# Scan stage: the step size's sums on GpSimd, two-source small VectorE steps, and a product of H and C that waits for its own scan

## What is computed

```python
x = L0_attn_x
x = x + 0.5 * _L0_ffn_ref(_layernorm(x, axis=-1), ...)
x = x + _L0_attn_ref(_layernorm(x, axis=-1), ...)
x = x + 0.5 * _L0_ffn_ref(_layernorm(x, axis=-1), ...)
x = x + 0.5 * _L1_ffn_ref(x, ...)
x = x + _L1_attn_ref(_layernorm(x, axis=-1), ...)
x = x + 0.5 * _L1_ffn_ref(x, ...)
```

```python
dt = jnp.einsum('blr,dr->bld', dt_low, W_dt)
delta = jax.nn.softplus(dt + b_dt)
A = -jnp.exp(A_log)

def step(h, inp):
    dlt_t, B_t, C_t, x_t = inp
    dA = jnp.exp(dlt_t[:, :, None] * A)
    h = h * dA + dlt_t[:, :, None] * B_t[:, None, :] * x_t[:, :, None]
    y_t = jnp.einsum('bdn,bn->bd', h, C_t)
    return (h, y_t)
```

## Time and profile before

| | us |
|---|---|
| times of three runs | 3141.8, 3126.4, 3141.92 |
| median | 3141.8 |
| span of the profiled execution | 3131.4 |
| scan stage, about | 1590 to 2772 |
| VectorE busy, whole span | 2073.9 |
| GpSimd busy, whole span | 1699.2 |
| TensorE busy, whole span | 2457.7 |

### The profile page before, as it was taken

How to read it: one execution, slowest core, us unless ns; L and a number is a source line. 1 busy time by engine, 2 the same in 40 slices (tenths; PEclk the granted TensorE clock), 3 DMA queues, 4 the chain that set the end, 5 groups by cost and what they waited for, 6 DMA issues and landing times. The chain is left out here.

```text
span 3131.4 us, 49074 instructions
## 1 busy us (share of the span) xinstructions
PE 2457.7 (78%) x12952; PEld 1742.2 (56%) x12952; DVE 2073.9 (66%) x6083; ACT 1589.5 (51%) x3093; POOL 1699.2 (54%) x1349
## 2 busy tenths in 40 slices
PE   4239996885799844399979888888888889769991
PEld 4239994664699733299933333333343334349991
DVE  6414445775444455155539999999999999955553
ACT  3115554773355443155545666666656666425550
POOL 5745550455355447555515566776666667645551
PEclk9999997996899976699989999999999999879996
DMA  9147771211677532477723344444433344337775
GB/s 330 53 129 229 225 228 59 68 52 42 197 229 227 158 109 72 123 227 226 228 83 129 129 135 141 141 137 137 137 128 130 136 136 144 104 115 228 226 228 171
DMA packets 268819, 479.26 MB, mean 153 GB/s; under 512 B 37453, under 2 KB 181803, under 8 KB 268560
## 3 DMA queue, kind: packets, MB, share of 16 engines
q1 hardware_dynamic: 225280, 405.41, 42.5%
q0 software_dynamic: 34816, 68.00, 6.1%
q10 hardware_dynamic: 8592, 4.33, 0.5%
HBM read 383.22 MB, written 98.54 MB: 154 GB/s over the span
## 5 line engine op out<-in xcount | busy, mean ns | idle before, releaser
L1736 POOL TENSOR_TENSOR ssm_HC<-ssm_H,ssm_BC 128x1024 f32<-128x1024 f32 x255 | 599.8, 2352 | 407.2 <-DVE ssm_psX L1806 338.3
L1492 PE MATMUL ssm_psY<-ssm_HC,ident 128*128 128x512 f32 x1020 | 517.4, 632 | 114.5 <-POOL ssm_HC L1736 114.3
L1650 ACT ACTIVATE ssm_dA<-ssm_delta,A 128x511 f32<-128x511 f32 x512 | 333.0, 710 | 189.1 <-DVE ssm_H L1815 119.9
L1492 PEld LDWEIGHTS ssm_psY<-ssm_HC,ident 128*128 128x128 f32 x1020 | 190.9, 197 | 382.1 <-POOL ssm_HC L1736 192.2
L1813 DVE TENSOR_TENSOR_SCAN ssm_H<-ssm_dA,ssm_psX 128x512 f32<-128x512 f32 x256 | 308.7, 1206 | 0.0
L1815 DVE TENSOR_TENSOR_SCAN ssm_H<-ssm_dA,ssm_psX 128x512 f32<-128x512 f32 x256 | 304.3, 1189 | 0.0
L471 POOL DMA_INDIRECT xslots<-att_r_xn,att_r_idx x128 | 128.3, 1002 | 178.5 <-DVE att_r_idx L451 140.4
L877 POOL DMA_INDIRECT a_back<-a_yr,a_to_row x144 | 139.8, 971 | 150.8 <-DVE a_yr L952 128.8
L877 POOL DMA_INDIRECT b_back<-b_yr,b_to_row x144 | 139.8, 971 | 150.6 <-DVE b_yr L952 128.6
L877 POOL DMA_INDIRECT d_back<-d_yr,d_to_row x144 | 139.8, 971 | 147.2 <-DVE d_yr L952 125.3
L877 POOL DMA_INDIRECT c_back<-c_yr,c_to_row x144 | 139.8, 971 | 144.7 <-DVE c_yr L952 121.0
(11 more groups left out here) (566 smaller groups left out, 5811.0 us busy)
## 6 DMA issues: line engine op xcount, KB each, us to landing
ssm_BC<-bc_rows SPq DMA_DIRECT2D x128, 1024.0 KB, 5.5
a_W<-in_l_pack SPq DMA_DIRECT2D x72, 514.0 KB, 3.4
b_W<-in_l_pack SPq DMA_DIRECT2D x72, 514.0 KB, 3.4
c_W<-in_l_pack SPq DMA_DIRECT2D x72, 514.0 KB, 3.4
d_W<-in_l_pack SPq DMA_DIRECT2D x72, 514.0 KB, 3.3
a_xs<-xslots SPq DMA_DIRECT2D x72, 131.0 KB
b_xs<-xslots SPq DMA_DIRECT2D x72, 131.0 KB
c_xs<-xslots SPq DMA_DIRECT2D x72, 131.0 KB
```

What stands on the lines that cost most here:

```text
L1492: last = nc.tensor.matmul(psY[:, dt, :], k.ident[:, :], HC[:, n % RP, dt, :], start=(n == 0), stop=(n == NB - 1))
L1650: last = nc.scalar.activation(dA[:, n % RA, dt, 1:], delta[:, b, dt, 1:], ACT.Exp, scale=A[:, dt, n:n + 1])
L1736: nc.gpsimd.tensor_tensor(HC[:, n % RP, :, :], H[:, n % RH, :, :], BC[:, n // CHUNK % SLOTS, 1, n % CHUNK:n % CHUNK + 1, :].to_broadcast([ ...
```

## The change

The three additions of the step size move from VectorE to GpSimd, where they stand between products: the correction after product 12, the logarithm after product 13, the relu after product 14 (for sequence 0, ahead of all products). ScalarE subtracts 1 again from 1 + u in one more instruction on 128 x 1024 numbers, so that GpSimd has plain two-operand instructions. Of the eight scatters, four stay behind products 8 to 11 and four move to products 0 to 3 of the next sequence. GpSimd's product no longer waits for `dBx_done`. Small one-source VectorE steps (scaling or adding a constant, two casts) become two-source ones, with rows of constants in SBUF as second source; the scaling of the mean (L211) is folded into later constants. The classes `Norm` and `Router` are used by the routing and attention stages too.

```diff
@@ Norm.dve_stats, Norm.dve_scales
-        nc.vector.tensor_scalar(m, m, 0.5, None, ALU.mult)
-        last = nc.vector.tensor_scalar(w[:, 0, :], v, EPS, None, ALU.add)
+        last = nc.vector.tensor_tensor(w[:, 0, :], v, self.k.eps[:, 0:T], ALU.add)
         if self.w == 2:
-            last = nc.vector.tensor_scalar(w[:, 1, :], v, 1.0 + EPS, EPS * EPS, ALU.mult, ALU.add)
+            last = nc.vector.scalar_tensor_tensor(out=w[:, 1, :], in0=v, scalar=1.0 + EPS, in1=self.k.eps_eps[:, 0:T], op0=ALU.mult, op1=ALU.add)
@@ Router.dve_0
-            last = nc.vector.tensor_scalar(n.rstd[:, 0, 0:T], n.rstd[:, 0, 0:T], 0.5, 1.0, ALU.mult, ALU.add)
+            last = nc.vector.scalar_tensor_tensor(out=n.rstd[:, 0, 0:T], in0=n.rstd[:, 0, 0:T], scalar=0.5, in1=k.ones_row[:, 0:T], op0=ALU.mult, op1=ALU.add)
-        nc.vector.tensor_scalar(self.rows(s, b)[:, :, D], k.token[:, bass.ds(t0, T)], 1.0, None, ALU.mult)
+        nc.vector.tensor_tensor(self.rows(s, b)[:, :, D], k.token[:, bass.ds(t0, T)], k.zeros[:, 0:T], ALU.add)
@@ Router.dve_2c
-        nc.vector.tensor_copy(self.ids(s, b), row.rearrange("p t c -> p (t c)")).then_inc(self.rowed, 1)
+        nc.vector.tensor_tensor(self.ids(s, b), row.rearrange("p t c -> p (t c)"), k.zeros[:, 0:TOPK * T], ALU.add).then_inc(self.rowed, 1)
@@ scan_stage, ScalarE: soften
                 nc.scalar.activation(rest[:, :, :], soft, ACT.Identity, bias=1.0).then_inc(one_ready, 1)
+                act.wait_ge(one_ready, s + 1)
+                nc.scalar.activation(rest[:, :, :], rest[:, :, :], ACT.Copy, bias=-1.0).then_inc(less_ready, 1)
@@ scan_stage, GpSimd
+            def correct(s):
+                pool.wait_ge(less_ready, s + 1)
+                nc.gpsimd.tensor_tensor(rest[:, :, :], soft, rest[:, :, :], ALU.subtract).then_inc(rest_ready, 1)
+            def lengthen(s):
+                pool.wait_ge(l_ready, s + 1)
+                pool.wait_ge(rest_ready, s + 1)
+                nc.gpsimd.tensor_tensor(rest[:, :, :], absv, rest[:, :, :], ALU.add).then_inc(sized, 1)
+            def sum_up(s, b):
+                pool.wait_ge(sized, s + 1)
+                pool.wait_ge(v_ready, s + 1)
+                nc.gpsimd.tensor_tensor(delta[:, b, :, :], rest[:, :, :], v[:, :, :], ALU.add).then_inc(delta_ready, 1)
                     pool.wait_ge(h_ready, s * NB + n + 1)
-                    pool.wait_ge(dBx_done, s * NB + n + 2)
...
-                    if n >= 8 and there(s - 2):
-                        R.pool_one(pool, s - 2, s % 2, n - 8)
+                    if n < 4 and there(s - 3):
+                        R.pool_one(pool, s - 3, 1 - b, n + 4)
+                    if 8 <= n < 12 and there(s - 2):
+                        R.pool_one(pool, s - 2, b, n - 8)
+                    if n >= 12 and not after:
+                        R.pool_one(pool, s - 2, b, n - 8)
+                    if n == 12 and after:
+                        correct(s + 1)
+                    if n == 13 and after:
+                        lengthen(s + 1)
+                    if n == 14 and after:
+                        sum_up(s + 1, 1 - b)
```

33 lines of the change are left out of this document (12 added, 21 removed).

## The result

The changed kernel takes 3349.64 us (median of 4 runs, 3348.62 to 3352.58); the kernel before, run beside it, 3135.74 (4 runs, 3126.4 to 3141.92). The ratio is 1.0686, with a 95% interval from 1.0662 to 1.071. Forecast were 3343 us and 1.064: the change makes the kernel slower, and the time lies within 0.2% of the forecast.

The account below looks back on a forecast made before the run. VectorE was taken to set the scan stage's pace, busy 68.85 of 69.91 us a sequence. Terms of 158.4 + 6.8 + 10.0 + 14.6 + 8.2 + 3.6 = 201.6 us on span 3131.4, plus 10.4, gave 3343 us; range 3240 to 3380.

Parts of the forecast that it names:

- The lock and its extrapolation: Scan stage: VectorE steps with two SBUF inputs are held until GpSimd's product ends; overlaps seen were under 1 us.
- Part 1: Steps 0 to 12: products waiting for h_ready alone hold small VectorE steps in eight steps; net +11.3 us a sequence.
- Part 2: Turn of the sequence: three sums on GpSimd make it 22.0 us in place of 20.09, +1.9 us.
- The row of six GpSimd instructions without a gap: At the turn: three sums and products 13, 14 and 15 follow one another on GpSimd, which becomes what is late.
- T(12): T(n) is the end of step n's second scan, when h_ready is signalled; zero point of the turn's computed times.
- the mean of two: End of the turn: T(0) at 22.3 if product 15 precedes L1772, 21.7 if L1772 is first; 22.0 taken.
- The added ScalarE copy: Turn: ScalarE's extra instruction of about 1.06 us was called hidden, since L407 ends 4.3 us after T(12).
- The other terms: Sequence 0 +6.8 us, sequence 1 +10.0, sequence 14 +14.6, sequence 15 +8.2, start +3.6, other stages 0.
- The median: Whole kernel: the runs' median, 3141.8 us, lies 10.4 above the profiled span of 3131.4; this offset was kept.
- Not held: First rival: small two-source steps are not held by a product that has just begun; 3119 us, chance 0.12.
- partly held: Second rival: holds are partial, half of the price, +100 us; 3242 us, chance 0.07.
- The third: Third rival: steps held twice as products follow without a gap, another 1.8 us in steps 8 to 12; 3387 us, chance 0.05.

Follow-up runs that it names:

- e11: The changed kernel with GpSimd's wait for dBx_done put back for product 13 alone; ratio 1.0616 to the kernel before.
- e1: The kernel before with only GpSimd's product no longer waiting for dBx_done, small steps in their old forms; 3346.25 us, ratio 1.0663.
- e12: The changed kernel with GpSimd's wait for dBx_done put back for products 13 and 14; ratio 1.0597 to the kernel before.
- e2: The changed kernel with the wait for dBx_done kept and small steps in their old one-source forms; 3152.86 us, ratio 1.0050 to the kernel before.
- e4: The changed kernel with the small steps of slots A and B issued between a step's two scans; 3150.98 us, ratio 1.0042 to the kernel before.
- e13: The kernel before with TensorE's gather earlier, scatters respread, mean scaling folded, ScalarE's router exponential ahead of the logarithm; 3244.45 us against 3276.07, ratio 0.9910.
- e3: The kernel before with only the changed kernel's Norm and Router (small steps' new forms, mean scaling dropped); 3137.16 us, ratio 0.9996.

## Why the prediction was right

**The lock and its extrapolation.** It stood on overlaps of under 1 us; they went on with slope 1 to overlaps of 1.9. Reductions (L419, 0.17 us) and steps with a PSUM operand (L401, 0.18) kept their durations beside a product.

**Part 1, +11.3 us a sequence: measured +10.96** (steps 0 to 12, mean of sequences 2 to 13: 61.08 against 50.12). The prices stand almost singly: computed 1.85, 1.85, 0.26, 1.71, 1.72, 1.85, 1.54 (1.74 less the 0.2 for L232) and 1.85 for steps 1 and 3 to 9; the steps grew by 1.80, 1.80, 0.18, 1.66, 1.67, 1.81, 1.49 and 1.79 us. Step 2 is 6.65 us in eleven of these twelve sequences (7.0 in one) in place of 6.7 to 9.0, the gain of 1.2 us that was counted against it. Steps 10 to 13 didn't change.

**Part 2, the turn, +1.9 us: measured +3.7.** This is the term that was mis-sized: 23.97 us against 22.0. The row of six GpSimd instructions without a gap was not there: four follow one another, then GpSimd idles. The timeline of VectorE, then GpSimd, in the changed kernel's turn (T(12) is 2448.50):

```profile
2453.46 4.88 DVE L417 TENSOR_TENSOR ssm_r_work<-ssm_r_prob,ssm_r_pv 128x32 f32<-128x32 f32 x1
...
2466.04 1.23 DVE L1790 TENSOR_TENSOR ssm_ux<-ssm_delta,ssm_xc 128x1024 f32<-128x1024 f32 x1
...
2451.34 2.35 POOL L1736 TENSOR_TENSOR ssm_rest<-ssm_pre,ssm_rest 128x1024 f32<-128x1024 f32 x1
2453.64 2.34 POOL L1757 TENSOR_TENSOR ssm_HC<-ssm_H,ssm_BC 128x1024 f32<-128x1024 f32 x1
2455.94 2.34 POOL L1741 TENSOR_TENSOR ssm_rest<-ssm_pre,ssm_rest 128x1024 f32<-128x1024 f32 x1
2461.36 2.35 POOL L1757 TENSOR_TENSOR ssm_HC<-ssm_H,ssm_BC 128x1024 f32<-128x1024 f32 x1 [3.08 <-DVE ssm_H L1833]
...
2466.07 3.40 POOL L1757 TENSOR_TENSOR ssm_HC<-ssm_H,ssm_BC 128x1024 f32<-128x1024 f32 x1
```

The step behind L416 was to be released with the first sum (here 2453.69). It is passed over there and again at the end of product 13 (2455.98), and ends with the second sum, at 2458.34. That is so in six turns (sequences 7 to 11 and 14). In seven others (2 to 6, 12 and 13) L417 comes 0.5 to 0.7 us after the first sum's end, meets product 13 alone and is passed over once. Either way it ends with the second sum, so T(14) comes at T(12) + 12.78 and not + 10.04; product 14, which waits for it, leaves GpSimd idle for 3.08 us; the third sum ends at + 17.5 and not + 15.07. From there on the forecast held: L1790 and product 15 come together (0.03 us apart), and T(0) follows 6.46 us after T(15), where 7.1 was computed.

e11 settles it: in its turns where the exponential is on time, nothing is passed over and the turn takes 22.4 us, the order in which product 15 comes first, for which 22.3 was computed. So 1.5 of the 2.0 us are the passing over. The other 0.4 is that this order always came, where I had taken the mean of two. That the sums were moved is not what makes the turn long, though: in e1, with the sums still on VectorE, it takes 23.7 us, since products 13 to 15 there meet VectorE's own sums and L1771, the product by x.

**The added ScalarE copy** (1.06 us, as estimated) was called hidden. L418 was put at T(12) + 4.24, but the reduction ahead of it reads the exponential, which ends at + 4.33 even in the kernel before: this was a misreading. L417 starts at + 4.96 at the earliest. It starts at + 5.9 in some turns for a reason that the prediction didn't look at. ScalarE's instructions ahead of the exponential wait for two matmuls of TensorE (L1467), which take 2.07 us in sequence 3 and 1.12 in sequence 9; the granted clock beside them is 0.50 and 1.00, the lower level (1.2 GHz) and the upper (2.4). In sequence 3 it fell at 1930.2, while TensorE idled from 1928.21 to 1930.58, as it had done from 1922.66 to 1924.99; in sequence 9 it was low from 2435.4 to 2438.8 and back when the pair came:

```profile
1930.58 2.07 PE L1467 MATMUL ssm_psA<-ssm_low,Wdt 64*128 64x512 f32 x2 [2.37 <-ACT ssm_v L1632]
2440.82 1.12 PE L1467 MATMUL ssm_psA<-ssm_low,Wdt 64*128 64x512 f32 x2 [1.48 <-ACT ssm_v L1632]
...
1930.50:1932.70 2.20, 2.12 (x3) 0.61 (x3) 2.20 (x4) 0.71 (x3) 2.06 (x2) 0.50 0.48 164
2440.80:2442.00 1.20, 1.18 (x3) 0.42 (x4) 1.20 (x2) 0.66 (x2) 1.12 (x2) 1.00 0.14 55
```

In all turns of the changed kernel and of e12 the exponential comes later the longer these two matmuls last; in the kernel before they are short in every turn (its two late exponentials have another cause). In the changed kernel this costs nothing, since L417 ends with the second sum in any case; where it is late in e11 and e12 it costs 0.8 us a turn. In e2 the pair is short in every turn and the exponential ends at T(12) + 5.4, which is + 4.3 and the copy: there the copy isn't hidden, and the wait of 1.75 us a turn costs the gain of a sum.

**The other terms.** Sequence 0 +5.6 us (computed 6.8), sequence 1 +10.3 (10.0), sequence 14 +15.6 (14.6), sequence 15 up to its last scan +7.6 (8.2), the start +4.1 (3.6). With 12 x 14.68 = 176.2 for the full sequences (158.4 computed) they add up to 219.4, just the difference of the spans, 3350.8 - 3131.4; 201.6 were computed. The other stages gave nothing, as assumed.

**The median.** Here a second, opposite miss of 11.6 us hid two thirds of the first, which was 17.8; that the forecast came within 7 us is luck to that extent. The 10.4 us between the span and the median of the kernel before were kept as an offset. The profiled execution of the kernel before was one of its shorter ones, though (its times go from 3126 to 3142), while the changed kernel's four runs lie within 4 us of each other and its median, 3349.6, lies 1.2 us under the span. With every term at its measured size I would have forecast 3361.

**The rivals.** "Not held" and "partly held" would have shown small steps of 0.15 or 1 us: L238's median is 1939 ns, and e4 takes the holds away by their place alone. The third, twice held steps, came true in its form (one step under two boundaries) but at the turn and not in steps 8 to 12, which take 5.4 and 3.42 us as computed.

## What to carry to other kernels

Before a wait is taken away because an engine idles in it, look at what that engine will then run beside: here 338 us of idle GpSimd cost nothing, and 2.35 us products that start 1.3 us earlier cost 11 us a sequence. Small two-source VectorE steps are not small beside a GpSimd instruction that reads SBUF, so they belong where none runs (e4), and the price can be computed from the timeline as the rest of the GpSimd instruction, but only if GpSimd stops after it. To find real gain, look at who waits for VectorE's inputs, not at who idles: exchanging queue entries of TensorE, GpSimd and ScalarE (e13) gave 0.9% with one small instruction a sequence less, whose loss alone was worth nothing measurable in e3. Of these 31.6 us the stage's trace explains 18.4.
